# Two-layer graph network: more gathered tiles moved from GpSimd to ScalarE and SyncE

## What is computed

```python
edge_index = jnp.stack([src, dst])                 # 106,250 edges, sorted by dst; 6250 nodes of 128 features
h = jnp.maximum(_layernorm(x), 0.0)
# layer 0
m = (h @ W.T + b)[src] * edge_weight[:, None]
x = x + jax.ops.segment_sum(m, dst, num_segments=6250)
# layer 1
h = jnp.maximum(_layernorm(x), 0.0)
msg_input = jnp.concatenate([h[src], h[dst]], axis=1)
for t in range(4):                                  # edge types
    m = jax.nn.relu(msg_input @ W1[t] + b1[t]) @ W2[t] + b2[t]
    msgs = msgs + jnp.where((edge_type == t)[:, None], m, 0)
agg = jax.ops.segment_sum(msgs, dst, num_segments=6250)
# a GRU cell of agg (gates W_ih) and h (gates W_hh) gives the layer's output, added to x
```

## Time and profile before

| | |
|---|---|
| runs | 2101.10, 2102.64, 2107.06 us; median 2102.64 |
| profiled execution | 2097.47 us, its span 2095.6 us |
| granted TensorE clock, mean | 0.743 |
| GpSimd | 1557.0 us busy (74%), 1648 instructions |
| TensorE matmul / weight load | 1286.6 (61%) / 1091.4 us (52%) |
| VectorE | 901.8 us (43%) |
| ScalarE | 570.4 us (27%) |
| DMA | 214.88 MB, mean 103 GB/s |

### The profile page before, as it was taken

How to read it: one execution, slowest core, us unless ns; L and a number is a source line. 1 busy time by engine, 2 the same in 40 slices (tenths; PEclk the granted TensorE clock), 3 DMA queues, 4 the chain that set the end, 5 groups by cost and what they waited for, 6 DMA issues and landing times.

```text
span 2095.6 us, 30265 instructions
## 1 busy us (share of the span) xinstructions
PE 1286.6 (61%) x6646; PEld 1091.4 (52%) x6646; DVE 901.8 (43%) x2555; ACT 570.4 (27%) x1508; POOL 1557.0 (74%) x1648
## 2 busy tenths in 40 slices
PE   2445445545455545456566676777777677777776
PEld 2434334434343433344356666666666666676665
DVE  7732232232232232232334555454555555555555
ACT  4723333333333333333331111111111111111111
POOL 7777777777777777777567777777777777777775
PEclk7666666666666566666768888888888888788888
DMA  8333323233333333333244444444444444444442
GB/s 183 120 81 92 87 81 101 78 82 99 80 81 100 79 81 92 87 81 99 76 123 113 108 116 113 113 114 116 113 113 117 113 113 117 114 110 118 115 111 70
DMA packets 182079, 214.88 MB, mean 103 GB/s; under 512 B 56480, under 2 KB 128043, under 8 KB 181394
## 3 DMA queue, kind: packets, MB, share of 16 engines
q0 software_dynamic: 52320, 107.26, 21.1%
q1 hardware_dynamic: 121836, 103.18, 17.1%
q10 hardware_dynamic: 7738, 2.46, 0.5%
HBM read 176.32 MB, written 36.41 MB: 102 GB/s over the span
## 4 chain that ended last, share of the span: by engine, by line
POOL 42%; issue 14%; ACTq 2%; PE 1%; ACT 1%; DMA 0%; DVE 0%; POOLq 0%; SPq 0%; DVEq 0%
POOL G L1745 15%; POOL edge L1745 15%; POOL g_more L1745 7%; POOL accs L1365 5%; ACTq L460 1%; PE bank L1672 0%; ACT accs L1541 0%; ACTq L439 0%; PE bank L1635 0%; PE bank L1650 0%; DMA edge<-p_tab,src_t 0%; DMA accs<-h_tab,src_t 0%; PE bank L1951 0%; DMA p_tab<-hot 0%; PE bank L1938 0%
## 5 line engine op out<-in xcount | busy, mean ns | idle before, releaser
L1365 POOL DMA_INDIRECT accs<-h_tab,src_t x762 | 719.6, 944 | 232.4 <-issue 231.2
L1927 PE MATMUL bank<-qwin,hotT 128*128 128x128 f32 x1662 | 295.1, 332 | 285.3 <-DVE hotT L1810 269.9
L1635 PE MATMUL bank<-accs 128*125 128x133 f32 x1662 | 342.1, 379 | 202.4 <-ACT accs L1541 155.1
L1635 PEld LDWEIGHTS bank<-accs 128*125 128x125 f32 x1662 | 318.7, 280 | 250.2 <-issue 145.7
L1927 PEld LDWEIGHTS bank<-qwin,hotT 128*128 128x128 f32 x1662 | 249.6, 230 | 325.0 <-DVE hotT L1810 306.3
L1745 POOL DMA_INDIRECT G<-p_tab,src_t x329 | 312.6, 950 | 118.6 <-issue 100.0
L1745 POOL DMA_INDIRECT edge<-p_tab,src_t x328 | 311.1, 949 | 100.1 <-issue 100.1
L1541 ACT ACTIVATE accs<-accs,edge 128x128 f32<-128x128 f32 x762 | 244.6, 390 | 465.6 <-issue 403.6
L1938 PE MATMUL bank<-hot,rows 128*128 128x128 f32 x1662 | 289.0, 332 | 6.0 <-ACT rows L1880 5.9
L1880 ACT ACTIVATE rows<-rows 128x512 f32<-128x512 f32 x208 | 130.7, 629 | 554.7 <-DVE rows L1820 527.9
L1938 PEld LDWEIGHTS bank<-hot,rows 128*128 128x128 f32 x1662 | 269.9, 246 | 9.0 <-ACT rows L1880 8.9
(11 more groups left out here) (179 smaller groups left out, 1285.0 us busy)
## 6 DMA issues: line engine op xcount, KB each, us to landing
w1a<-p_tab ACTq DMA_DIRECT2D x1674, 0.5 KB
qwin<-q_tab SPq DMA_DIRECT2D x416, 64.0 KB
hotT<-h_tab ACTq DMA_DIRECT2D x1546, 0.5 KB
nodew<-key_tab SPq DMA_DIRECT2D x52, 256.0 KB
nodehot<-key_tab SPq DMA_DIRECT2D x52, 256.0 KB, 3.5
accs<-h_tab,src_t POOLq DMA_INDIRECT x762, 2.5
p_tab<-st SPq DMA_DIRECT2D x25, 224.0 KB
p_tab<-hot SPq DMA_DIRECT2D x25, 224.0 KB
```

The source lines that it names most:

```text
L1365: eng.indirect_dma_start(slot0(o % R0)[:, t, 0:D], None, table, bass.IndirectOffsetOnAxis(src_t[:, k:k + 1], 0)).then_inc(s_g0[o % R0][t / ...
L1635: ins = eng.matmul(pb[SUM_BANK[o % 4]][0:CW, 0:FW], ones_of(o % HR)[:, t, :], slot0(o % R0)[:, t, :], start=t == 0, stop=t == last)
L1927: ins = eng.matmul(pb[2 + g % 2][:, t * D:(t + 1) * D], hotT[:, g % HT, t * P:(t + 1) * P], qwin[:, g % NG, t // PR, :], start=True, stop= ...
```

## The change

ScalarE fetches 14 tiles of layer 0 by rows instead of 12, over the same 180 half octets, and 15 of layer 1 instead of 13, over the same 196 groups. SyncE fetches 3 tiles of layer 0 by rows, shared over 91 octets from step 6, in a loop that otherwise only stores tables; before that loop it now waits for the row numbers and for `h0_tab` to be stored. GpSimd skips these tiles: 5 fewer in layer 0, 2 fewer in layer 1.

```diff
         TAIL0, TAIL1 = ((NTILE - 1, [(o, 0, E - (NTILE - 1) * P)]) for o in (194, 202))
-        rows_act0 = ByRow("act", spread(12, 14, 180, 2, TO, TO - 2) + [TAIL0],
+        rows_sp0 = ByRow("sp", spread(3, 6, 91, 1, TO, TO - 1),
+                         lambda j: hotT[:, 2, (2 + j % 2) * D:(3 + j % 2) * D], hotT[0:1, 0, P:3 * P].bitcast(I32))
+        rows_act0 = ByRow("act", spread(14, 14, 180, 2, TO, TO - 2) + [TAIL0],
                           lambda j: hotT[:, 2, j % 2 * D:(1 + j % 2) * D], hotT[0:1, 1, P:3 * P].bitcast(I32))
-        rows_act1 = ByRow("act", spread(13, 2, 196, 1, GT, GT - 1) + [TAIL1],
+        rows_act1 = ByRow("act", spread(15, 2, 196, 1, GT, GT - 1) + [TAIL1],
                           lambda j: w1a[:, j % 2, :], w1b[0:1, 0:2, :].rearrange("p a d -> p (a d)").bitcast(I32), rows_act0)
-        alone0, alone1 = ({k: (rows, j) for j, (k, _) in enumerate(rows.tiles)}
-                          for rows in (rows_act0, rows_act1))
-        assert NTILE == NT - 1 and NTILE % GT == 3 and len({k // GT for k in alone1}) == len(alone1) == 14 and len(alone0) == 13
+        alone0, alone1 = ({k: (rows, j) for rows in who for j, (k, _) in enumerate(rows.tiles)}
+                          for who in ((rows_sp0, rows_act0), (rows_act1,)))
+        assert NTILE == NT - 1 and NTILE % GT == 3 and len({k // GT for k in alone1}) == len(alone1) == 16 and len(alone0) == 18
...
+            eng.wait_ge(s["row_st"], 32)
+            row_numbers(eng, rows_sp0, 0, place_tab0)
+            eng.wait_ge(s["tab"], 32 * len(T_PIECES))
             for o in range(STEPS0 + 1):
                 for p, i in units_at(o):
                     if i == 1:
                         p_rows_out(p)
                     if i == 2:
                         q_rows_out(p)
+                rows0(eng, rows_sp0, o)
```

## The result

| | before | changed |
|---|---|---|
| runs, us | 2101.10, 2102.64, 2103.68, 2104.13, 2107.06 | 2162.01, 2169.33, 2171.87, 2172.41, 2172.99 |
| median | 2103.68 | 2171.87 |
| profiled execution (span) | 2097.47 (2095.6) | 2171.87 (2169.7) |
| GpSimd / ScalarE busy | 1557.0 / 570.4 | 1554.8 / 566.8 |

The changed kernel is slower: ratio 1.0306, 95% interval 1.0291 to 1.0320, which is 64 us (61 to 67); the two medians lie 68 us apart. The two profiled executions differ by 74 us, since that of the kernel before was 6 us under its median. 73 of these 74 us lie before layer 1's first gather.

The account below looks back on a forecast made before the run. ScalarE's row issuing, nearly level with GpSimd before, was to pace layer 0. Profiled 2097.5 us, plus 77 (92 later, 15 given back), minus 2.5 in layer 1, is 2172; half of 5.2 added, 2175. Range 2167 to 2189; 8 in 10, 2150 to 2196.

Parts of the forecast that it names:

- ScalarE has about 10 us to spare in layer 0: Layer 0, 140 to 975 us: only about 10 us in 835 of ScalarE's idle time was real waiting for gathers.
- A row tile is 51.1 us of sequencer: ScalarE: 128 row DMAs at 0.321 us plus four address loads at 2.5 us; layer 0's two more tiles cost 102.3 us.
- `root` 43 us apart: Layer 0: `root` instructions of successive units on ScalarE come 43 us apart, where two before stood 38.5 apart.
- GpSimd waits some 60 us for TensorE, from about 440 us on: Layer 0: after some 35 us of lag GpSimd waits for slots; its wait grows from 1.2 to about 60 us.
- The layer's end gives back 15 us (12 to 18): Layer 0's last octets: late ScalarE finds gathers landed and catches up 15 us, so layer 1 begins 77 us later.
- SyncE's rows cost nothing and save nothing: Layer 0: SyncE's 153 us of issuing hides in its waits; gathers saved are worth nothing while ScalarE sets the pace.
- Layer 1 gains 2.5 us: Layer 1: GpSimd paces it, ScalarE's added rows hide, and two gathers fewer gain 2.5 us (bounds 0 and 2.5).
- GpSimd stays the bound: Rival, both layers: the rows hide in ScalarE's idle time and the kernel gets faster, 2089 us; chance 0.06.
- The slots swallow the lag: Rival, end of layer 0: ScalarE and TensorE catch up fully, layer 1 waits only on GpSimd's delay, 2152 us; chance 0.10.
- SyncE pushes ScalarE aside: Rival, layer 0: SyncE's issues delay ScalarE's, up to 123 us more; at a third of that 2215 us; chance 0.05.
- layer 1 tips over: Rival, layer 1: ScalarE's 102 us of added issuing show there too, 2277 us; chance 0.03.

Follow-up runs that it names:

- e6: Kernel before with 13 instead of 12 tiles of layer 0 on ScalarE, nothing else added: 2124.14 us against 2103.36, ratio 1.0098.
- e5: Kernel before with only SyncE's three row tiles of layer 0 added: 2100.09 us against 2103.36, ratio 0.9985.
- e10: Kernel before with only ScalarE's layer 1 tiles raised from 13 to 15: 2098.17 us against 2099.56, ratio 0.9990.
- e11: Layer 0 with 11 tiles on ScalarE and 12 on SyncE, layer 1 with 15 on ScalarE; slower chip: 2814.72 us against 2697.11 for the kernel before.
- e9: Changed kernel with five octet slots instead of six: 2172.38 us against 2099.56 for the kernel before, ratio 1.0341.
- e1: Kernel before with only SyncE's three row tiles of layer 0 added, on a slower chip: 2711.19 us against 2657.07, ratio 1.0194.
- e3: Kernel before with only ScalarE's layer 1 tiles raised from 13 to 15, on a slower chip: 2676.58 us against 2657.07, ratio 1.0077.

## Why the prediction was right

Forecast 2175, measured 2171.87, inside the range; the likeliest case was the one that came. The closeness of the sum is in part luck: layer 1 began 73.0 us later and not 77, and then took 1.1 us more and not 2.5 less, and the two misses cancel to within 1 us (74.1 against 74.5). By its steps:

- *ScalarE has about 10 us to spare in layer 0.* Right. In the changed kernel its waits for gathers are gone from 140 us on, and octet 97 came 91.4 us later, where 102.3 - 10 was forecast; e6 with one tile leaves 51.1 - 42.0 = 9 us of slack. One tile more already costs 21 us there.
- *A row tile is 51.1 us of sequencer.* Right: ten rows span 3.40 us (a pitch of 0.35 there; 0.32 without the slower first issues), a load has a median of 2.24 us, and the step from 13 to 14 tiles moved layer 1 by 49.9 us. The shortest load here, with ten addresses instead of 32, took 1167 ns. The Trainium skill ("DMA: Bandwidth & Descriptors", "Latency and other measured facts") gives about 600 ns as the floor of a `tensor_load`. No load here contradicts that, but it was no price for these: the sum had to go by the trace's 2.25 us.
- *`root` 43 us apart.* Right: 42.4 in the pair shown (978.45 to 1020.84), and 43.5 on average over layer 0's first 22 spacings (109.93 to 1066.11), where the kernel before has 39.4 (108.99 to 975.36). Single spacings vary by some 2 us either way.
- *GpSimd waits some 60 us for TensorE, from about 440 us on.* The amount is right (63.8 us). The begin is not: the first long stall is at 560 us. The lag grew nearly as forecast (the `root` that stood at 463.58 came 33.8 us late, that at 542.27 42.4 us). The term that was mis-sized is what the slots already had in use: I took 35 us of further lag before they run out, and they held 42 to 45. One piece of it was also misread: the weighing at 1036.94 is that of the last tile, which ScalarE fetches by rows; the last gather (1033.82) was weighed from 1036.34 on, 2.5 us after its start and not 3.1. It changed nothing in the sum, since the end of the layer follows ScalarE.
- *The layer's end gives back 15 us (12 to 18).* 18.8, just above the upper bound. With the gathers landed, ScalarE lost little to TensorE, 2.29 us at L1562.
- *SyncE's rows cost nothing and save nothing.* No harm shows in e5, where they are worth about 3 us. In the changed kernel itself, where GpSimd waits anyway, their part was not taken apart from the rest; the median of ScalarE's row DMAs is 231 ns there as in the kernel before.
- *Layer 1 gains 2.5 us.* Not seen in the pair of traces: from the first gather of the layer to the end it was 1043.4 us instead of 1042.3. e10 alone gave 0.2 to 4.0 us. Its ScalarE had room, as forecast; the size stays open.
- The rivals: *GpSimd stays the bound* would have meant 2089 and fell. The Trainium skill (same page, "Issuing engines are not separate DMA queues") sets the time to initiate a DMA against the DMA itself and calls it usually small. The nearest rows don't contradict the sentence: in e11, on a slow chip, ScalarE's wait ended 1.2 to 1.4 us after the last row DMA of SyncE in nine of the ten tiles it waited for, and the pitch is 0.32 us. What failed is the step from there to rows that cost almost nothing: sent one by one, 128 times a tile, the small time fills the sequencer. *The slots swallow the lag* fell in e6 and by e9's trace, *SyncE pushes ScalarE aside* in e5, *layer 1 tips over* in e10. On the chips with 2657 and 2697 us the last two come nearer to what was measured (e1 54 us slower; e3 12 to 29 us); such chips weren't in the forecast at all.

## What to carry to other kernels

An engine that issues many small DMAs is busy although its busy share says 27%: count its issues times their pitch, and see what ended its idle stretches before giving it more. Work belongs where both the engine and the stretch have room: here SyncE with 12 tiles and ScalarE with 10 beat the changed kernel's 3 and 14 by 3.6% (0.9948 against 1.0306, each beside its own kernel before), on the chips that take 2100 us. A ring of buffers hides a lag only from the engine that fills it; whatever waits for the end of the stage still pays.

## What the runs showed that I had not expected

The same kernel took 2100 us on one chip and 2657 and 2697 us on two others. Comparing e5 and e1, the durations of gathers are the same (the kernel before has a median of 0.944 us, e1 0.947), the granted clock of 300 to 900 us differs little (0.64 in e5, 0.61 in e1), and the DMA engines were less busy. What differs is the sequencers of ScalarE and SyncE: in e1 single MOVEs and DMA_DIRECT2Ds of their rows took up to 1.45 us, in e5 at most 0.04 and 0.64, and ScalarE's MOVEs add up to 344 us instead of 94. With it the sign of a change can flip: SyncE's three tiles gave -0.15% on one chip and +1.9% on another.

What slows them was not tested, and the cause is open. The fetching of instructions is a candidate, but the traces don't point at it. e1 has 193 packets on the DMA queues for instructions and e5 191, with the same medians (1.0 us on one queue, 0.43 to 0.44 on the other), while e1 has 861 row instructions of over 0.6 us and e5 one. And TensorE, whose list is longer than either, has no such stumbles: its longest instruction takes 1.22 us in e1 and in the kernel before.
